# Eight single banks in a ring for the maxima's pass of two attention blocks, the other products dealt out between its steps

## The reference

```python
def _L1_attn_ref(h, q_w, q_b, k_w, k_b, v_w, v_b, o_w, o_b):   # H = 16 heads of 16, B, S = 4, 256
    q = (h @ q_w.T + q_b).reshape(b, s, H, HEAD_DIM)
    k = h @ k_w.T + k_b                                        # one key and value head for all
    v = h @ v_w.T + v_b
    scores = einsum('bqhd,bkd->bhqk', q, k) / HEAD_DIM ** 0.5
    attn = softmax(where(causal, -inf, scores))
    return einsum('bhqk,bkd->bqhd', attn, v).reshape(b, s, H * HEAD_DIM) @ o_w.T + o_b

def _L2_xattn_ref(x, y, ...):                                  # B = 4 batches of 256 tokens, 16 heads of 16
    y_dca, y_main = y[:, -16:, :], y[:, :-16, :]               # 240 main keys and 16 of the second context
    k_dca, v_dca = _ln(y_dca @ Wk_dca + b), y_dca @ Wv_dca + b
    q, k, v = _ln(x @ Wq + bq), _ln(y_main @ Wk + bk), y_main @ Wv + bv
    return (_attn(q, k, v) + _attn(q, k_dca, v_dca)) @ Wo + bo
```

## Time and profile before

| | |
|---|---|
| profiled execution | 2233.82 us, of it span 2231.7 us |
| median of three runs | 2229.27 us |
| PE busy | 1901.9 us (85%), 9078 products |
| DVE busy | 1229.9 us (55%) |
| ACT busy | 786.9 us (35%) |
| POOL busy | 258.3 us (12%) |
| maxima's pass of `MultiQuery` | 493.6 to 532.4 us |
| maxima's pass of `TwoContexts` | 1146.5 to 1197.0 us |

### The profile page before, as it was taken

The page is one execution under the profiler, slowest core; times in us unless marked ns, Lnnn a source line. Parts: engine busy times, 40 slices in busy tenths (PEclk is TensorE's granted clock), DMA queues, the critical chain, the costliest instruction groups (busy, mean ns, idle before and its releaser), DMA issues.

```text
span 2231.7 us, 25452 instructions
## 1 busy us (share of the span) xinstructions
PE 1901.9 (85%) x9078; PEld 1210.3 (54%) x9078; DVE 1229.9 (55%) x2789; ACT 786.9 (35%) x1864; POOL 258.3 (12%) x244
## 2 busy tenths in 40 slices
PE   5684776978669699999998778999999899998698
PEld 3451222545555366666666545555555477777355
DVE  5738998746663444444466585333334566765221
ACT  4215444302342133333443322333333455554111
POOL 2711000000104300000000200000000222220111
PEclk9796887989869799999987989999999899998799
DMA  3001000000442200000100123000002000002310
GB/s 148 1 5 52 0 0 20 1 29 1 185 192 79 97 1 1 1 1 1 38 1 1 67 86 132 1 1 1 0 1 84 32 1 1 1 1 85 94 33 13
DMA packets 17371, 83.13 MB, mean 37 GB/s; under 512 B 3136, under 2 KB 10052, under 8 KB 13152
## 3 DMA queue, kind: packets, MB, share of 16 engines
q1 hardware_dynamic: 11168, 71.35, 8.1%
q0 software_dynamic: 2944, 8.03, 1.2%
q10 hardware_dynamic: 3136, 2.13, 0.3%
HBM read 73.23 MB, written 8.81 MB: 37 GB/s over the span
## 4 chain that ended last, share of the span: by engine, by line
PE 73%; DVE 15%; issue 6%; POOL 3%; ACT 2%; DMA 1%; POOLq 0%; SPq 0%; DVEq 0%; ACTq 0%
PE bank L136 59%; PE bank L141 8%; PE bank L3526 3%; DVE space L795 2%; PE bank L3548 2%; DVE space L784 1%; DVE space L1359 1%; DVE space L3039 1%; DVE space L178 1%; DMA space<-in_L_attn 1%; POOL space L625 1%; POOL space L639 1%; DVE space L272 0%; DVE space L189 0%; DVE space L2387 0%
## 5 line engine op out<-in xcount | busy, mean ns | idle before, releaser
L136 PE MATMUL bank<-space 128*128 128x256 f32 (+16 forms) x6734 | 1468.6, 423 | 73.3 <-ACT space L822 10.3
L136 PEld LDWEIGHTS bank<-space 128*128 128x128 f32 (+7 forms) x6734 | 896.7, 181 | 597.4 <-issue 394.7
L141 PE MATMUL bank<-consts,space 128*128 128x128 f32 (+2 forms) x1602 | 255.4, 301 | 170.8 <-DVE space L189 50.1
L141 PEld LDWEIGHTS bank<-consts,space 128*128 128x128 f32 (+2 forms) x1602 | 202.9, 153 | 237.7 <-issue 125.5
L136 PE MATMUL bank<-space,consts 128*128 128x512 f32 (+2 forms) x150 | 95.1, 761 | 59.7 <-DVE space L790 50.3
L197 POOL TENSOR_TENSOR space<-space,consts 128x4 f32<-128x4 f32 x22 | 24.9, 1132 | 686.4 <-DVE space L184 686.4
L2623 POOL TENSOR_TENSOR space<-space,consts 128x4 f32<-128x4 f32 x64 | 68.5, 1071 | 220.7 <-DVE space L2554 220.7
L2418 ACT ACTIVATE space<-bank,space 128x256 f32<-128x256 f32 x128 | 59.4, 469 | 95.7 <-DVE space L2372 95.7
L2372 DVE TENSOR_REDUCE space<-bank 128x2 f32<-128x512 f32 x64 | 44.0, 688 | 87.0 <-PE bank L136 86.8
L136 PEld LDWEIGHTS bank<-space,consts 128*128 128x128 f32 (+1 forms) x150 | 29.9, 225 | 104.9 <-DVE space L790 71.5
L3526 PE MATMUL bank<-space 128*128 x176 | 81.1, 605 | 3.1 <-DVE space L3676 3.1
(11 more groups left out here) (350 smaller groups left out, 1948.3 us busy)
## 6 DMA issues: line engine op xcount, KB each, us to landing
space<-in_L_ffn SPq DMA_DIRECT2D x13, 2048.0 KB, 11.9
space<-in_L_attn SPq DMA_DIRECT2D x10, 2048.0 KB, 13.2
space<-in_L_xattn SPq DMA_DIRECT2D x4, 2048.0 KB, 10.1
expert_results<-space SPq DMA_DIRECT2D x16, 128.0 KB, 3.4
space<-expert_results SPq DMA_DIRECT2D x8, 256.0 KB, 4.7
space<-in_L_xattn SPq DMA_DIRECT2D x1, 1919.0 KB, 19.3
space<-in_L_xattn SPq DMA_DIRECT2D x1, 1536.0 KB, 6.2
space<-in_L_attn SPq DMA_DIRECT2D x1, 1074.5 KB, 5.1
```

What stands on the lines that cost most here:

```text
L136: return self.nc.tensor.matmul(out, lhsT, rhs, start=first, stop=last, skip_group_check=True)
L141: return self.nc.tensor.transpose(out, src, eye)
```

## The change

In both blocks each bank that the pass needs becomes a **place** in one list, `PLACES`, in the order in which the steps write them, and place `n` is bank `n % 8`. A step waits for what stood at place `n - 8` and for that alone (`wait_bank`). So a unit can be written whole while the unit before is read, where nothing else stands between; the turns have no banks of their own any more.

In `TwoContexts` the steps beside are cut up: one tile of `keys`, `queries` or `values` (one bank) is a step, and one or two of them stand behind each of the units 0 to 7; `second_keys`, the two halves of `second_values` and `bias` stand behind units 8 to 11. The first two tiles of keys now come ahead of unit 1 and take the wait for `centred.all`. The scores' semaphore is counted by each of a unit's four banks, and DVE waits for each bank by itself. In `MultiQuery` the second pass begins with a wait for all maxima. The instructions and their sizes stay, and so do the second passes.

```diff
 class MultiQuery(Stage):
-    RING1, RING2 = 6, 6
+    RING2 = 6
+    FIRST = [(kind, at) for u in range(19) for kind, at in (("turn", u // 4 - 1), ("scores", u))
+             if (kind == "turn" and u >= 6 and u % 4 == 2) or (kind == "scores" and u < 16)]
+    PLACES = [(kind, at, j) for kind, at in FIRST for j in range(4 if kind == "scores" else 2)]
...
+    def bank(self, *place):
+        return self.c.banks[self.PLACES.index(place) % 8]
+    def wait_bank(self, e, *place):
+        n = self.PLACES.index(place) - 8
+        if n >= 0:
+            kind, at, j = self.PLACES[n]
+            e.wait_ge(*(self.s.maxed(4 * at + j + 1) if kind == "scores" else self.s.q_done(at + 1)))
...
     def scores(self, e, u):
-        mine = [bk[(4 * u + j) % self.RING1] for j in range(4)]
+        mine = [self.bank("scores", u, j) for j in range(4)]
         for j in range(4):
-            n = 4 * u + j
-            if n >= self.RING1:
-                e.wait_ge(*s.maxed(n - self.RING1 + 1))
+            self.wait_bank(e, "scores", u, j)
...
     def scores_turned(self, e, u):
+        if u == 0:
+            e.wait_ge(*s.maxed.all)
...
 class TwoContexts(Stage):
-    BESIDE = {1: ("keys", 1), 2: ("queries", 1), 3: ("values", 0), 4: ("second_keys", 0), 6: ("second_values", 0), 7: ("bias", 0)}
+    BESIDE = {0: [("keys", 0), ("keys", 1)], 1: [("keys", 2), ("keys", 3)], 2: [("queries", 0), ("queries", 1)],
+              3: [("queries", 2), ("queries", 3)], 4: [("values", 0)], 5: [("values", 1)], 6: [("values", 2)], 7: [("values", 3)],
+              8: [("second_keys", 0)], 9: [("second_values", 0)], 10: [("second_values", 1)], 11: [("bias", 0)]}
...
+    PLACES = [(kind, at, j) for kind, at in FIRST for j in range({"scores": 4, "turn": 2}.get(kind, 1))]
...
-            scores=16, maxed=64, ...
+            scores=64, maxed=64, ...
...
+    def wait_bank(self, e, *place):
+        t, n = self.t, self.PLACES.index(place) - 8
+        if n < 0:
+            if n >= -4:
+                e.wait_ge(*self.s.centred.all)
+            return
+        kind, at, j = self.PLACES[n]
+        if kind == "scores":
+            e.wait_ge(*t.maxed(4 * at + j + 1))
+        elif kind == "turn":
+            e.wait_ge(*t.q_done(at + 1))
+        elif kind == "keys":
+            e.wait_ge(*t.late_tile(at + 1))
...
     def scores(self, e, u):
-        if p == 1:
-            e.wait_ge(*self.s.centred.all)
...
-        done.then_inc(*t.scores.one)
+                if i == TPB - 1:
+                    done.then_inc(*t.scores.one)
...
     def maxima(self, e):
             elif kind == "scores":
-                e.wait_ge(*t.scores(at + 1))
...
                 for j in range(4):
+                    e.wait_ge(*t.scores(4 * at + j + 1))
```

More of the change, by code:

```diff
@@ L1234, in tensor @@
         N = len(self.UNITS)
[L1235 to L1239, removed]
+        for kind, at in self.FIRST:
+            (self.turn_rows if kind == "turn" else self.scores)(e, at)
         for u in range(N + 3):
@@ L1345, in vector @@
         N = len(self.UNITS)
-        for u in range(N + 3):
-            if u >= 6 and (u - 6) % 4 == 0:
-                b = (u - 6) // 4
+        for kind, u in self.FIRST:
+            if kind == "turn":
+                b = u
                 e.wait_ge(*s.rows_turned(b + 1))
@@ L1351, in vector @@
                     q = self.q[:, 2 * m:2 * m + 2, b * S:(b + 1) * S]
-                    done = nc.vector.tensor_tensor(q, q, bk[6 + m].rearrange("p (a b) -> p a b", b=S), ALU.add)
+                    done = nc.vector.tensor_tensor(q, q, self.bank("turn", b, m).rearrange("p (a b) -> p a b", b=S), ALU.add)
                 done.then_inc(*s.q_done.one)
-            if u < N:
+            else:
                 b, f = self.UNITS[u]
@@ L2773, in attention @@
         N = len(self.UNITS)
[L2774 removed]
+        for kind, at in self.FIRST:
             if kind == "scores":
[L2776 removed]
+                self.scores(e, at)
             elif kind == "turn":
[L2778 removed]
+                self.turn_rows(e, at)
             else:
[L2780 removed]
+                self.beside(e, kind, at)
         n = 0
@@ new lines, in wait_bank @@
+    def wait_bank(self, e, *place):
[11 more added lines that the diff above has]
+            e.wait_ge(*t.late_tile(at + 1))
+        elif kind == "queries":
+            e.wait_ge(*t.late_tile(at + 5))
+        elif kind == "values":
+            e.wait_ge(*t.v_ready(at + 1))
+        elif kind == "second_keys":
+            e.wait_ge(*t.dca_ready.all)
+        elif kind == "second_values":
+            e.wait_ge(*t.vd_ready(at + 1))
+        else:
+            e.wait_ge(*t.bias_ready.all)
@@ L2806, in wait_half, with beside @@
+    def beside(self, e, kind, at):
+        c, w, s, t = self.c, self.w, self.s, self.t
+        bank = self.bank(kind, at, 0)
+        if at == 0:
+            if kind == "keys":
+                e.wait_ge(*s.centred(4))
             elif kind == "queries":
-                e.wait_ge(*t.late_tile(j + 5))
-            elif kind == "values":
-                e.wait_ge(*t.v_ready(j + 1))
+                e.wait_ge(*s.centred(9))
             elif kind == "second_keys":
-                e.wait_ge(*t.dca_ready.all)
+                e.wait_ge(*s.centred(5))
@@ L2812, in wait_half @@
             elif kind == "second_values":
[L2813 to L2820, removed]
+                e.wait_ge(*s.many_ready.all)
+            elif kind == "bias":
+                e.wait_ge(*s.scaled.all)
+        self.wait_bank(e, kind, at, 0)
         if kind in ("keys", "queries"):
[L2822 to L2825, removed]
+            self.turn_tile(bank, NT + 4 if kind == "keys" else 4, at).then_inc(*t.late_mm.one)
@@ L2826, in beside @@
         elif kind == "values":
[L2827 to L2832, removed]
+            for j in range(2):
+                from_ = at * S + j * self.KT
+                done = c.mm(bank[0:self.KT, j * D:(j + 1) * D], w["ctxT"][:, 0, from_:from_ + self.KT], w["Wv"][:, 0, :])
@@ L2841, in beside @@
[L2841 to L2845, removed]
-        else:
-            e.wait_ge(*s.scaled.all)
-            self.wait_half(e, p, 3)
+            for j in range(2):
+                done = c.mm(bank[:, j * D:(j + 1) * D], self.many[:, 2 * at + j, :], w["Wvd"])
+            done.then_inc(*t.vd_mm.one)
+        else:
@@ L3134, in scalar @@
                                  repeat(w["dcaT"][:, n * DCA:(n + 1) * DCA], P // DCA), ACT.Copy).then_inc(*s.many_ready.one)
-        for p, (kind, _) in enumerate(self.FIRST):
-            self.take_beside(e, kind, self.half_of_banks(p))
+        for kind, at in self.FIRST:
+            if kind not in ("scores", "turn"):
+                self.take_beside(e, kind, at, self.bank(kind, at, 0))
         for u in range(len(self.UNITS)):
```

72 lines of the change are left out of this document (32 added, 40 removed).

## The result

The changed kernel takes 2207.4 us (median of six runs, 2203.3 to 2212.0). Of the six runs of the kernel before in the same comparison one was slow, with 2597.5 us, and isn't counted; the median of the other five is 2229.3 us. The profiled execution took 2212.0 us, 2210.0 of it span; it was the slowest of the six.

What follows compares the result with a forecast made beforehand. The banks were taken to bound the passes, and behind them DVE. Gains of 3.9 us in MultiQuery and 8.2 in TwoContexts made 12.1, which off the median of 2229.3 gave 2217 us, range 2211 to 2223.

Steps and rivals of the forecast that it cites:

- The loop of 2.40 us: TwoContexts, units 0 to 4: each period 2.40 us, 0.13 over DVE's 2.27; first unit to fifth 9.6 us.
- The sum for the passes: Both passes: 3.9 us gained in MultiQuery and 8.2 us in TwoContexts, together 12.1 us.
- the term for the gathers: MultiQuery: three gathers between units at 0.44 us each, 1.32 us of a pass of 34.8 us.
- the count for each bank: TwoContexts: handing banks over sooner saves 0.03 us a unit, one issue gap more costs 0.04; taken as zero.
- turns 1.19 instead of 1.24: TwoContexts, units 4 to 15: three turns on DVE at 1.24 us each, 3.72 us.
- bias 0.33 instead of 0.41: TwoContexts, units 4 to 15: the bias adds at most 0.41 us on DVE.
- Everything behind just starts sooner: After the passes: last turn and second pass unchanged, no transfer waited for, what follows only moves earlier.
- 2220 to 2222: Clock rival: PE left waiting and a longer low stretch behind the pass give back 2 to 4 us; chance 0.22.
- 0.03 for a gain: Chance left for a low-clock stretch that shortens, with a time of 2211 to 2214 us.
- PE's half clock inside the passes: Rival for both passes: PE at half clock makes them 10 + 12 us longer, time 2251 us; chance 0.03.
- No place was late: Rival, strict list: one late place stops PE; TwoContexts gains 4 us instead of 8.2, time 2221 us; chance 0.10.
- The slower case: Rival with PE at half clock through both passes, time 2251 us; chance 0.03.

## Why the prediction was wrong

**Direction and mechanism of the passes: right.** DVE doesn't wait in either, the turns cost no idle time, and the wait ahead of the first maximum of `MultiQuery` is 3.33 us as before. The loop of 2.40 us that was put at units 0 to 4 of `TwoContexts` is the one part of the mechanism that didn't hold.

**The sum for the passes: 12.1, measured 13.5.** In `MultiQuery` the term for the gathers was too large: from 492.03 to 499.76 are sixteen maxima (four times 1.86) and one gather, 0.29 us, not 0.44. The 0.44 came from a unit without idle time that PE was nevertheless bounding; three times 0.15 is the 0.5 us that were missing. In `TwoContexts` the term of 2.40 us for units 0 to 4 was 2.26, because I gave the count for each bank "0.03 us a unit" where it takes the whole loop off the path; that is 0.5 of the 0.9 us. The rest is terms taken at their upper bound: turns 1.19 instead of 1.24, bias 0.33 instead of 0.41.

**The pass of before was taken from one execution.** The sum set the new passes against 38.7 and 50.5 us. These were the old passes on good terms with the clock; others had 41.4 and 52.6. I had seen that PE's masks and scores stood in the old rounds, but not drawn the consequence: such a round gets longer at half clock. 1.2 us more in the mean.

**"Everything behind just starts sooner": the step that failed.** I weighed the clock as something that takes back, "2220 to 2222", and called the shift's effect something that could go either way, with 0.03 for a gain. The sum so put every block behind the passes at nothing: 12.1 us of gain, all of it in the passes. Measured were 24, of which the passes are 13.5 to 14.7 and untouched blocks some 10. The shift doesn't average out, since the program is in step with the raster when it comes to the passes (0.70 to 0.86 us behind a line in all fourteen profiles). The feed-forward block behind `MultiQuery` took 105.0 to 107.8 us in five of the six profiles with the new pass and no delay, and 109.9 to 113.1 in the three with the old one, and a delay of 0.93 us takes 8 us away. The delays show that the place counts for several us, and in both directions. That the shift of this change fell on the good side was luck: nothing in the prediction works out its direction.

**What stays open.** 14.7 us for the passes and some 5 for that block leave 4 to 5 of the 24 us. Other untouched blocks come in two lengths as well (344.3 or 342.1 us for the block from 1372.72 us of the kernel before, and 334.9 or 332.4 for the one behind it, once 333.8), and old and new kernels had both. Which length comes goes with the place at the block's start (the table above), but one or two profiles for each kernel can't say how often a kernel has which. So this remainder isn't accounted for.

**The rivals.** PE's half clock inside the passes cost nothing: in `TwoContexts` 0.94 and 0.97 over the pass gave the same 41.41 us. The clock as a whole gave time where the rival said that it takes some. No place was late: idle time ahead of the maxima of `TwoContexts` is 0.0 us. The slower case didn't come near.

## What to carry to other kernels

In a ring, count how many banks stand free between a reader's step and its writer's next; where the loop through the last bank is longer than the slower engine's work, that difference is idle time, and it grows when the other engine's clock falls. Let each bank be handed over by itself, and cut work that stands beside into pieces of one bank. When a whole kernel moves by more or less than the stretch that was changed, compare blocks that weren't touched, and add a plain delay of a few tenths to a few us in several lengths: if the time doesn't rise with the delay, the total measures the place as well (here the place against the clock's steps), and a change of a few us can't be judged by the total alone.

## What the runs showed of the hardware

A kernel that waits 2.3 us longer was faster (0.9964, 0.9940 to 0.9987), and one that waits 0.93 us longer was 8 us slower than without. TensorE's granted clock changes on an even raster (within 0.001 us in each of fourteen traces) that doesn't start with the program: its start stands 0.29 to 2.89 us behind a line. This program comes into step with it: 490 us on, the first maximum of `MultiQuery` stands 0.70 to 0.86 us behind a line in all fourteen.

Filling 3.3 us of idle PE with transposes nobody reads kept the clock at 1.00 through the following 64.75 us; left idle, the same work took up to 69.0 us at 0.91. In the other thirteen traces PE idles 2.4 to 6.0 us ahead of the last turn of each of the two passes, and runs the turn or what follows it at half clock each time.

A matrix product held up by its bank doesn't hold up the products before it on other strips of the array: in the changed kernel three of them ended up to 0.23 us before the fourth (1148.20 and 1148.43 us), and the reader began at 1148.35.
